# The eighth probability tile of each softmax sum moves from TensorE to an accumulating DMA, in a two-layer attention kernel

## The reference: what is computed

```
xn  = group_norm(x, gamma, beta)                    # 32 groups
q, k, v = split(einsum('oc,bcn->bon', w_qkv, xn) + b_qkv)
m   = softmax(einsum('bct,bcs->bts', q * s, k * s), axis=-1)   # 8 heads, 1024 x 1024 each
a   = einsum('bts,bcs->bct', m, v)
out = x + einsum('oc,bcn->bon', w_proj, a) + b_proj
```

## Time and profile before

| | |
|---|---|
| median of 3 runs | 2149.19 us (2148.03 to 2149.98) |
| the profiled execution, its own time | 2149.15 us |
| its span, first to last instruction | 2147.4 us |
| mean granted TensorE clock | 0.99 of full |
| PE busy | 2092.4 us (97%) |
| POOL busy | 1791.0 us (83%) |
| DVE busy | 1696.5 us (79%) |
| ACT busy | 1238.8 us (58%) |
| 16 DMA engines, packets of the hardware queue | 32.0% of the span |

### The profile page before, as it was taken

How to read it: one execution, slowest core, us unless ns; L and a number is a source line. 1 busy time by engine, 2 the same in 40 slices (tenths; PEclk the granted TensorE clock), 3 DMA queues, 4 the chain that set the end, 5 groups by cost and what they waited for, 6 DMA issues and landing times.

```text
span 2147.4 us, 37263 instructions
## 1 busy us (share of the span) xinstructions
PE 2092.4 (97%) x10552; PEld 1160.0 (54%) x10552; DVE 1696.5 (79%) x2896; ACT 1238.8 (58%) x2321; POOL 1791.0 (83%) x567
## 2 busy tenths in 40 slices
PE   5999999999999999999999999999999999999998
PEld 3455555555555555555555555555555555556542
DVE  3878888788887888887887888878887788888881
ACT  2355656566565665656565565655656556565654
POOL 2398988888887988978988888978889889889895
PEclk8799999999999999999999999999999999999999
DMA  4333243322334233244322434223343222433211
GB/s 125 60 57 63 61 100 80 92 44 59 84 80 100 62 68 65 65 100 99 85 50 52 98 79 99 55 56 70 80 99 75 70 56 60 99 80 80 54 27 40
DMA packets 208741, 157.04 MB, mean 73 GB/s; under 512 B 166528, under 2 KB 166784, under 8 KB 208512
## 3 DMA queue, kind: packets, MB, share of 16 engines
q1 hardware_dynamic: 208512, 154.48, 32.0%
HBM read 36.39 MB, written 16.78 MB: 25 GB/s over the span
## 4 chain that ended last, share of the span: by engine, by line
PE 90%; POOL 4%; issue 2%; DVE 2%; SPq 1%; ACT 1%; DMA 1%; DVEq 0%; ACTq 0%; POOLq 0%
PE ps_t L396 23%; PE ps_m L421 21%; PE ps_v L442 21%; PE ps_d L464 10%; PE ps_m L456 6%; PE ps_d L479 5%; PE ps_d L472 5%; POOL acc L876 3%; DVE raw_max L708 1%; SPq L290 1%; ACT pt L631 0%; DMA qs<-neg_max 0%; PE ps_m L464 0%; DMA par<-pars_dram 0%; PE ps_t L487 0%
## 5 line engine op out<-in xcount | busy, mean ns | idle before, releaser
L631 ACT ACTIVATE pt<-ps_t 128x512 f32<-128x512 f32 x2048 | 1110.2, 599 | 835.2 <-PE ps_t L396 823.5
L708 DVE TENSOR_REDUCE raw_max<-ps_m 128x1 f32<-128x512 f32 x2048 | 1316.8, 685 | 304.7 <-PE ps_m L421 265.2
L876 POOL TENSOR_TENSOR acc<-acc,pt 128x2048 f32<-128x2048 f32 x317 | 1450.7, 4576 | 32.7 <-POOL gn_c L861 5.5
L421 PE MATMUL ps_m<-ks,qs 96*128 96x512 f32 x2048 | 994.1, 487 | 14.4 <-DVE raw_max L708 13.2
L396 PE MATMUL ps_t<-qs,ks 97*128 97x512 f32 x2048 | 842.9, 413 | 13.1 <-ACT pt L631 11.7
L396 PEld LDWEIGHTS ps_t<-qs,ks 97*128 97x128 f32 x2048 | 389.7, 190 | 379.3 <-ACT pt L631 158.6
L876 POOL TENSOR_TENSOR acc<-pt 128x2048 f32<-128x2048 f32 x64 | 292.7, 4573 | 264.8 <-ACT pt L631 264.8
L421 PEld LDWEIGHTS ps_m<-ks,qs 96*128 96x128 f32 x2048 | 391.8, 191 | 193.2 <-DVE raw_max L708 115.0
L442 PE MATMUL ps_v<-pt,v 128*32 128x512 f32 x4096 | 492.7, 597 | 0.0
L464 PE MATMUL ps_d<-xn,wq 128*128 128x512 f32 x500 | 263.6, 611 | 5.8 <-ACT xn L663 5.8
L442 PEld LDWEIGHTS ps_v<-pt,v 128*32 128x32 f32 x4096 | 119.5, 109 | 250.4 <-issue 171.0
(11 more groups left out here) (49 smaller groups left out, 540.2 us busy)
## 6 DMA issues: line engine op xcount, KB each, us to landing
ks<-stage_kh SPq DMA_DIRECT2D x256, 128.0 KB, 2.4
qs<-stage_qh SPq DMA_DIRECT2D x256, 128.0 KB, 2.4
ks<-stage_kl SPq DMA_DIRECT2D x128, 128.0 KB, 2.4
qs<-stage_ql SPq DMA_DIRECT2D x128, 128.0 KB, 2.5
qs<-neg_max SPq DMA_DIRECT2D x1024, 0.5 KB, 2.0
xn<-x_dram SPq DMA_DIRECT2D x16, 512.0 KB, 4.5
res<-x_dram SPq DMA_DIRECT2D x16, 512.0 KB, 4.5
between<-res SPq DMA_DIRECT2D x32, 256.0 KB, 2.3
```

Of the source, the lines that this page charges most:

```text
L421: pe.matmul(ps_m[max_bank(u)][:, :], qs[b][0:KROWS, h, c:c + P], ks[b][0:KROWS, h, kf * HALF:(kf + 1) * HALF], start=True, stop=True).then ...
L631: act.activation(pt[t % 4][:, h, :], ps_t[score_bank(s.g, u)][:, :], ACT.Exp, scale=SCALE).then_inc(exp_done, 1)
L708: dve.tensor_reduce(raw_max[:, e % 2, t, kf:kf + 1], ps_m[max_bank(u)][:, :], AX.X, ALU.max)\
L876: pool.tensor_tensor(acc[hf][:, :, :], a[:, :, :], pt[t % 4][:, :, :], ALU.add).then_inc(pool_added, 1)
```

## The change

GpSimd now issues, after the six adds of a half, one DMA that adds the eighth tile onto acc in SBUF (`accum_op=ALU.add`, 128 rows of 8 KB, 1 MB). TensorE then takes the sums of acc alone, four products in place of eight, and does so 19 units into the next half (units 19 and 51) instead of 11. ScalarE's wait ahead of unit 12 is for the landing of that DMA. The last half of all keeps its five tiles. In the last slot only one piece of the output projection (LAST_PIECES) stands among the units, from step 6, and three follow at the end; before it was two and two, from step 5. GpSimd's program is written out in full (`write_slots`) instead of looping.

```diff
-SUMS_AT = 11
+SUMS_AT = 19
@@ sums (TensorE)
-                pe.wait_ge(pool_added, ADDS * half + pooled - 1)
+                if pooled == POOLED:
+
+                    pe.wait_ge(last_tile_added, 16 * (half + 1))
+                    tiles = [acc[hf]]
+                else:
+
+                    pe.wait_ge(pool_added, ADDS * half + pooled - 1)
+                    tiles = [pt[t % 4] for t in range(pooled, NT)] + [acc[hf]]
 
                 pe.wait_ge(max_done, reduced)
-                tiles = [pt[t % 4] for t in range(pooled, NT)] + [acc[hf]]
@@ slot, end (TensorE; VectorE alike)
-                elif not has_next and LAST_OUT <= step < LAST_OUT + CT:
+                elif not has_next and LAST_OUT <= step < LAST_OUT + LAST_PIECES:
...
-            for piece in range(CT, CT * NH):
+            for piece in range(LAST_PIECES, CT * NH):
@@ exp (ScalarE)
-                        act.wait_ge(sum_ready, half)
+                        act.wait_ge(last_tile_added, 16 * half)
@@ GpSimd
+            def add_last_tile(half, hf):
+
+
+                pool.wait_ge(exp_done, HG * (NT * half + NT))
+                pool.wait_ge(pool_added, ADDS * (half + 1))
+                pool.dma_start(acc[hf][:, :, :], pt[POOLED % 4][:, :, :], accum_op=ALU.add).then_inc(last_tile_added, 16)
@@ slot (GpSimd)
+                    if has_next or hf < NH - 1:
+                        add_last_tile(NH * s.n + hf, hf)
...
-            run_slots(pool, slot)
+            write_slots(slot)
@@
-LAST_OUT = 5
+LAST_OUT = 6
+LAST_PIECES = 1
```

More of the change, by code:

```diff
@@ L247, in attention_layers @@
         pool_added = sem("pool_added")
+        last_tile_added = sem("last_tile_added")
         sum_ready = sem("sum_ready")
@@ L785, in slot @@
                             v_out(s.j + 1, 1 - s.v, step)
-                    if part == 1 and not has_next and LAST_OUT <= step < LAST_OUT + CT:
+                    if part == 1 and not has_next and LAST_OUT <= step < LAST_OUT + LAST_PIECES:
                         project_out(s.j, step - LAST_OUT)
```

## The result

The changed kernel takes 2233.5 us (median of 4 runs, 2224.6 to 2241.73) against 2149.15 us for the kernel before beside it (4 runs, 2148.03 to 2149.98). The ratio is 1.0392 with an interval of 1.0351 to 1.0433: slower. The forecast was 2131 us and faster, with a range that ended at 2215, so the time lies outside the range too. The profiled execution took 2224.6 us with a span of 2222.5; it is the quickest of the four, and in the other three TensorE's mean clock is a little lower (0.960 to 0.965 against 0.969), so it understates the difference by some 9 us.

What follows compares the result with a forecast made beforehand. TensorE, busy 97%, was taken to set the pace: 2149.15 - 51.3 (sums removed) + 31 (TensorE standing behind D) + 2 (the end) = 2131 us. The 8-in-10 range was 2097 to 2215 us, the forecast's own 2108 to 2149.

Steps and rivals of the forecast that it cites:

- A: First of four recurring halves, following D; GpSimd idles 4.18 us; landing forecast 7.0 us, covered by a 9.0 us limit.
- D: Every fourth half, group norm between GpSimd's adds, 1.13 us idle; forecast TensorE standing 2.2 us in 14 such halves: 31 us.
- B: Half after A; GpSimd idles 3.98 us; landing forecast 7.5 us beside staging, covered by a 9.0 us limit.
- C: Half after B, before D; GpSimd idles 4.32 us; landing forecast 7.0 us, covered by a 9.0 us limit.
- For which I add 0.5: 7.5 us: Landing behind B and D: 7.0 us taken for the DMA, plus 0.5 for meeting the next slot's staging copies.
- That of 9.0 us: Limit behind A, B and C: landing up to 9.0 us after the adds costs TensorE nothing.
- That of 5.3 us behind D: Limit behind D: landing up to 5.3 us is free; beyond it TensorE stands microsecond for microsecond.
- 60 x 0.855 = 51.3 us: TensorE's gain: one tile's sums, 0.855 us, removed in 60 counted halves, 51.3 us.
- 2.55 us a half remain, so even 2.3 is hidden: GpSimd's idle time left per half, 2.55 us, hides the DMA's issue even at 2.3 us; 1.0 taken.
- Rival 3: GpSimd becomes the bound: issue takes 4.6 us, over its room by 2.05 in 60 halves; 2223 us; chance 0.07.
- Rival 2: Accumulation passes every byte twice, landing 10.0 us, 10.5 beside staging; TensorE stands 113 us; 2213 us; chance 0.30.
- Rival 1: Landing hidden everywhere, up to 5.3 us with the staging beside it; 2100 us; chance 0.15.

Runs made afterwards that it cites:

- 8: Changed kernel with the accumulating DMA cut to 512 KB, two of four heads (eighth tile of the others left out of the sums): 2131.49 us, ratio 0.9924.
- 3: Changed kernel with a plain copy of the same 1 MB to a scratch buffer instead of the accumulation, waited for alike: 2137.68 us, ratio 0.9958.
- experiment 7: Changed kernel with a buffer of its own for tile 7 and the residual's load moved from piece 1 to piece 5: 2115.76 us, ratio 0.9851.
- experiment 11: Changed kernel with own buffer for tile 7, residual loaded at piece 5 and VectorE's program written out: 2096.71 us, ratio 0.9751.
- 9: Kernel before with VectorE's program written out instead of a loop of four slots: 2132.99 us, ratio 0.9933.
- 10: Kernel before with sums at units 19 and 51, own buffer for tile 7, VectorE's program written out, no accumulating DMA: 2134.78 us, ratio 0.9938.
- 5: Kernel before with only GpSimd's program written out without a loop: 2148.05 us, ratio 0.9997.
- 1: Changed kernel with a buffer of its own for tile 7, so ScalarE's unit 12 no longer waits for the landing: 2135.25 us, ratio 0.9941.

## Why the prediction was wrong, by its own steps

The table shows where the 93 us between forecast and measurement lie, in us of span against the kernel before (negative is gained), by the periods of halves 2 to 59. The forecast's terms are 0.855 gained in each and the 31 us of standing in A:

| | forecast | measured | |
|---|---|---|---|
| A, behind D | +19.0 | +51.0 | landing and clock |
| B | -12.0 | -1.1 | VectorE's turns |
| C, behind B | -12.8 | +22.8 | landing and clock |
| D | -12.8 | -4.0 | GpSimd is the bound |
| the rest (start, last halves, end) | +0.3 | +6.4 | the last wait behind a D, and the end |
| sum | -18.3 | +75.1 | |

**"For which I add 0.5: 7.5 us" (the landing behind B and D): this step failed.** The landing, counted from the end of the adds as the prediction counted it, is 7.8 us behind A, 8.5 behind C, 9.2 behind D and 10.2 behind B. First, 0.55 us pass before GpSimd issues, and the forecast had nothing for them. Second, from issue it is 7.3 us behind A, 8.0 behind C, 8.6 behind D and 9.6 behind B, so traffic beside it adds 1.3 and 2.3 us to A's 7.3, not 0.5. Behind B it is the staging; behind D moving the staging away gave back only 0.4 to 0.6 us, and the rest of that cause stays open. B is of two kinds: where VectorE's loop turns the landing from the adds is 8.5 to 9.6 us, elsewhere mostly 11.0 to 11.8.

Third, "I stay nearer the lower end and take 7.0 us" is what an undisturbed DMA takes (the shortest is 7.1), but by luck. The shortest landings of experiments 8 and 3 are 4.6 us for half the bytes accumulated and 4.3 for the plain copy. That is 2.5 us for 512 KB and 2.1 fixed, so beyond the fixed part the copy of 1 MB takes 2.2 us and the accumulation 5.0, about twice. The forecast came to the same 5.0 as a little more than the 4.0 of the staging's 264 GB/s, a rate too low for this copy. Two errors cancelled.

The Trainium skill, "Collectives: The Full Stack", section "The bandwidth ceiling: the fold count and why AG ≠ RS ≠ AR", gives half the rate for an add in the DMA path, there of a ReduceScatter; experiments 3 and 8 agree (1.9 times beyond the fixed part). The Trainium skill, "DMA: Bandwidth & Descriptors", section "Anatomy of one DMA — SWDGE (gpsimd) path", has the formula that gave an estimated 4.4 us: the plain copy's shortest landing, 4.3 us, agrees, its median of 5.2 beside other transfers is longer, and the accumulation isn't covered by it.

**The limits.** That of 9.0 us held. Behind A (7.8) nothing stands: the next period is 31.00 us where no turn of VectorE's loop falls into it. Behind B the next period is 31.3 to 32.3 us for landings up to 9.6 us, and 34.0 to 37.6 for those from 11.0. That of 5.3 us behind D was about 1 us too tight: TensorE stands 2.9 us a time there for a landing of 9.2, which makes it 6.3. In experiment 7, where ScalarE doesn't wait for the landing, exponential 12 starts 5.5 us behind D's adds instead of 4.81. Against experiment 7, whose mean periods A and C are 31.1 and 31.3 us where those of the changed kernel are 35.6 and 33.7, D costs 4.5 us a time and B 2.4. TensorE's idle time behind unit 12 is 2.9 of the 4.5 and 1.4 of the 2.4; the lower clock withholds another 24 / 14 = 1.7 and 12 / 14 = 0.9, which accounts for both.

So "D is not, 31 us" was right in kind at half its size, 14 x 4.5 = 63, and "A, B and C are covered" was wrong for B, 14 x 2.4 = 33. (A slip of the sum: the forecast's own range begins at 2149.15 - 51.3 + 2 + 14 x 0.7 = 2110, not 2108.)

**A term was missing: the clock.** The prediction priced a stand microsecond for microsecond. Between experiment 7 and the changed kernel lie 108.9 us of span (the page of 7):

```profile
PE 2052.1 (97%) x10048; PEld 1140.5 (54%) x10048; DVE 1687.7 (80%) x2896; ACT 1238.5 (59%) x2321; POOL 1846.3 (87%) x630
```

TensorE's time not busy grows by (2222.5 - 2096.6) - (2113.6 - 2052.1) = 64.4 us, and its busy time by 2096.6 - 2052.1 = 44.5 us for the same matmuls. That second part is the lower clock: by the mean clocks it is 69 - (1 - 0.986) x 2113.6 = 39 us. So a stand of TensorE is paid for 1.6 to 1.7 times here. That the clock falls because of the stands is read from where it falls: in 11 of the 14 periods behind D and 6 of the 14 behind B, and in none of these in experiment 7. No run varied the clock alone. In B the stands are VectorE's turns, whose six periods are 35.3 to 36.6 us where 34.6 - 0.86 was due; there too the clock is lower, as in three of the six in experiment 7. The prediction said that the change leaves these turns as they are.

**"60 x 0.855 = 51.3 us" came out smaller.** With everything hidden (experiment 11 against 9, both without VectorE's turns) the gain is 2132.99 - 2096.71 = 36.3 us, against 51.3 - 2 = 49. In the timelines of 7 and of before, the periods A, B and C without a turn give 0.84 to 0.86 us each, exactly the tile of sums (every second A 1.1); D gives only 0.23 (32.40 to 32.17), since there GpSimd has become the bound. That is 14 or 15 x 0.63 = 9 of the missing 13 us. In the two profiled executions 2.6 us more lie ahead of GpSimd's first add, where the executions of these kernels differ by up to 6 us anyway; the rest isn't placed. The step at fault is "2.55 us a half remain, so even 2.3 is hidden": it averaged GpSimd's idle time over four halves. From the end of D's last add (1151.46) to the next first add (1152.65) are 1.2 us, 0.55 of them idle ahead of the issue. That is in the range taken, but D has 1.13 us idle of its own, of which TensorE's gain takes 0.86, and it can't borrow from A.

**What held.** The sums moved at next to no cost where VectorE's loop is written out (9 and 10), and GpSimd's loop went at none that shows (5). The end was 3.6 us and not 2: from the first add of the third last half on, the kernel before takes 93.7 us and the changed one 97.3. Rival 3 held in D alone and at a fraction of its price. Rival 2 had the mechanism, every byte priced twice, at 8.0 (median) instead of 10.0 us from issue. Its 2213 is near 2233.5 partly by chance, for it charged A and C, which hardly stand, and not the clock, which does cost. Rival 1's time, 2100, is reached in experiment 11 alone, with a third thing, VectorE's turns, taken off; without that it is 2116 (7).

**Also warned of, and not priced:** "if the DMA slows the row loads". In the changed kernel TensorE's stands hide it; it shows as soon as they are gone, as 20 us between experiments 1 and 7 by the medians (24 by the spans of the profiled executions, all of it in the periods C; that of experiment 1 is its slowest).

## What to carry to other kernels

Before handing work to a DMA, ask first when its result is needed and whether one more buffer can put that off: the same transfer cost 3.9% when unit 12 waited for it and gained 0.6% when unit 19 was the first, and 1.5% with the queue of the other transfers put in order. Price an accumulating DMA by its bytes at twice a copy's, plus what runs beside it, and slack by the single stage that has least of it, not by an average. Where TensorE is made to stand some microseconds again and again, look for what its clock loses afterwards: here some 0.6 to 0.7 us for each microsecond of standing.

## What was unexpected of the hardware

- An accumulating DMA of 1024 KB from SBUF to SBUF lands 8.0 us after issue (7.1 to 11.3), the plain copy after 5.2 (4.3 to 7.5), 512 KB accumulated after 5.0 (4.6 to 7.2). For the same packets and bytes the accumulation holds the DMA engines 1.9 times as long (5.4 and 2.8 us). Its issue holds GpSimd for 0.87 to 0.93 us, a plain copy's for 0.57, with 0.55 us of idle time ahead.
- While it is on its way, SyncE needs up to 6.84 us to issue four DMAs of 0.5 KB that take some 2.5 otherwise. The Trainium skill, "DMA: Bandwidth & Descriptors", section "Issuing engines are not separate DMA queues", says that the transfers of all engines run on the same 16 DMA engines, which agrees. The Trainium skill also says there that the time to issue is usually small relative to the DMA itself; that does not hold for these rows, 1.7 us each where the median landing of such a row is 2.1:

```profile
1084.25 0.87 POOL L890 DMA_DIRECT2D acc<-pt  x1 [0.55 <-ACT pt L638]
1087.24 6.84 SPq L301 DMA_DIRECT2D qs<-neg_max  x4
```

- VectorE's program written out gave 14.3 us (2147.3 - 2132.99, ratio 0.9933), where GpSimd's gave 0.9997. Each of the six turns of VectorE's loop is 3 us of issue, but by the spans (17.5 us) only 8.6 us of the gain lie in the six periods with a turn (34.6 to 33.2 us); 6.6 lie in the other periods A to C, and the rest is the difference of start and end. What else the written-out program saves VectorE isn't shown.
